# A gated state-space and feed-forward kernel on one core: the order of the feed-forward pieces inside the steps of the scan

## The reference

```python
# layer 1, for each sequence; z = layernorm(x)
u     = silu(conv(in_proj_w @ ctx) + conv_b)
dt_lo, Bm, Cm = x_proj_w @ u
delta = softplus(dt_proj_w @ dt_lo + dt_proj_b)
state = state * exp(delta_t * A) + (delta_t * u_t) * B_t      # over t, 256 channels x 16 states
y     = sum_n state * C_t;  y = (y + D * u) * silu(z)
x     = x + tanh(g_xattn) * y
# layer 2; act_quant: per token, scale = 128 / max|x|, rounded; weight_quant: ternary
h     = layernorm(x)
inter = silu(act_quant(h) @ wq_gate.T) * (act_quant(h) @ wq_up.T)
x     = x + tanh(g_ffn) * (act_quant(fwht(inter)) @ wq_down.T)   # fwht: Walsh-Hadamard over 1024
```

## Time and profile before

| | us |
|---|---|
| median of 3 runs (lowest, highest) | 287.43 (285.79, 288.03) |
| the profiled execution's own time | 287.4 |
| its span, first to last instruction | 285.6 |
| DVE busy (share of the span) | 211.9 (74%) |
| PE busy | 202.8 (71%) |
| ACT busy | 157.5 (55%) |
| POOL busy | 146.9 (51%) |
| mean granted clock of TensorE, as a share of full speed | 0.831 |

### The profile page before, as it was taken

One profiled execution on the slowest core, in us unless ns is written; L12 is line 12 of the kernel. 1 busy time (PEld: TensorE's weight loads), 2 busy tenths in 40 slices (PEclk: granted clock), 3 DMA queues, 4 the chain that ended last, 5 costly groups with the idle time before them and its releaser, 6 DMA issues. The chain is left out here.

```text
span 285.6 us, 3700 instructions
## 1 busy us (share of the span) xinstructions
PE 202.8 (71%) x1216; PEld 164.9 (58%) x1216; DVE 211.9 (74%) x340; ACT 157.5 (55%) x271; POOL 146.9 (51%) x213
## 2 busy tenths in 40 slices
PE   3779499936796976478595865695959646493856
PEld 2467389924684964367484743484848435372744
DVE  4399997839999984659696946497969355669872
ACT  1677979594045969732866579115773600651140
POOL 1101954999620685599795054999300098306600
PEclk9999755985797799989869599779886959979595
DMA  2990000000000000000000000000000000000001
GB/s 55 297 346 11 0 3 0 1 2 0 0 0 2 0 1 2 1 0 0 2 0 18 0 3 0 18 1 2 0 18 2 1 0 21 0 0 1 18 21 37
DMA packets 8149, 6.34 MB, mean 22 GB/s; under 512 B 2202, under 2 KB 7874, under 8 KB 8130
## 3 DMA queue, kind: packets, MB, share of 16 engines
q1 hardware_dynamic: 7154, 6.02, 6.5%
q10 hardware_dynamic: 976, 0.09, 0.2%
HBM read 5.05 MB, written 1.05 MB: 21 GB/s over the span
## 5 line engine op out<-in xcount | busy, mean ns | idle before, releaser
L1094 POOL TENSOR_SCALAR driveT<-duT,BT 128x256 f32<-128x256 f32 x120 | 61.1, 531 | 41.5 <-ACT duT L828 17.2
L811 ACT ACTIVATE decay<-delta,zero_c,aneg 128x255 f32<-128x255 f32 x128 | 65.4, 588 | 4.4 <-DVE state L1219 2.7
L458 PE MATMUL PY<-id,prod 128*128 128x128 f32 x256 | 44.3, 331 | 3.4 <-DVE prod L1261 1.9
L404 PE MATMUL BC<-id,driveT 128*128 128x128 f32 x120 | 23.4, 330 | 31.0 <-DVE state L1219 31.0
L458 PEld LDWEIGHTS PY<-id,prod 128*128 128x128 f32 x256 | 39.2, 175 | 5.4 <-issue 2.3
L1119 POOL TENSOR_TENSOR wnat<-wnat 128x512 f32<-128x512 f32 x18 | 22.8, 1267 | 36.8 <-DVE wnat L1341 36.0
L1219 DVE TENSOR_TENSOR_SCAN state<-decay,BC 128x512 f32<-128x512 f32 x30 | 36.4, 1212 | 3.5 <-issue 3.1
L1261 DVE TENSOR_TENSOR prod<-state,BC 128x1024 f32<-128x1024 f32 x32 | 38.2, 1195 | 0.0
L404 PEld LDWEIGHTS BC<-id,driveT 128*128 128x128 f32 x120 | 17.1, 174 | 34.1 <-issue 27.0
L1219 DVE TENSOR_TENSOR_SCAN state<-decay,UP 128x512 f32<-128x512 f32 x30 | 35.8, 1194 | 0.0
L1341 DVE SCALAR_TENSOR_TENSOR wnat<-GP,us,wq 128x1024 f32<-128x1024 f32 x7 | 9.0, 1283 | 30.0 <-issue 30.0
(11 more groups left out here) (205 smaller groups left out, 409.0 us busy)
## 6 DMA issues: line engine op xcount, KB each, us to landing
wnat<-in_L_ffn_w_gate_dram SPq DMA_DIRECT2D x1, 1024.0 KB, 9.6
xs<-in_x_dram SPq DMA_DIRECT2D x1, 1024.0 KB, 12.0
wnat<-in_L_ffn_w_up_dram SPq DMA_DIRECT2D x1, 1024.0 KB, 11.9
wnat<-in_L_ffn_w_down_dram SPq DMA_DIRECT2D x1, 1024.0 KB, 11.3
out_dram<-ot SPq DMA_DIRECT2D x8, 128.0 KB, 1.7
ctxs<-in_ctx_dram SPq DMA_DIRECT2D x1, 384.0 KB, 7.1
ctxs<-in_ctx_dram SPq DMA_DIRECT2D x1, 128.0 KB, 2.9
inw<-n_L_xattn_in_proj_w_dram SPq DMA_DIRECT2D x1, 128.0 KB, 2.7
```

Source lines behind the costliest of these rows:

```text
L404: last = nc.tensor.transpose(drive_bank(h)[:, L * n + P * c:L * n + P * (c + 1)], driveT[:, m % RING, c, n, P * h:P * (h + 1)], id32[:])
L458: last = nc.tensor.matmul(PY[:, E * c + P * h:E * c + P * (h + 1)], prod[:, g % RING, h, n, P * c:P * (c + 1)], id32[:], is_transpose=True ...
L811: last = nc.scalar.activation(decay[:, m % RING, h, n, 1:L], delta[:, b % 2, h, 1:L], ACT.Exp, bias=zero_c[:], scale=aneg[:, h, NB * j + n ...
L1094: last = nc.gpsimd.tensor_scalar(driveT[:, m % RING, c, n], duT[:, b % 2, c], BT[:, b % 2, c, NB * j + n:NB * j + n + 1], 1.0, ALU.mult, A ...
```

## The change

The order of pieces inside the steps changes on DVE, PE and ACT; POOL's and SP's programs stay, and so do the number and the shapes of all instructions. On DVE several pieces now stand between the scans and the product of a step instead of ahead of the scans or behind the product; the product comes later in these steps. On PE tokens_T moves ahead of `C_rows` of step 3, the gates go to step 3, up 0 to step 4, up 1 and down 1 to step 5, q2_T and down of half 0 one step later. On ACT rstd2 goes to step 1, the silus to step 3 behind its decays, tokens_out_early ahead of them, and q2_out_early 0 behind the decays of step 2. For f = 0 the transposed tokens go to bank6 instead of X, and four waits are changed to fit the new order.

```diff
--- before.py
+++ after.py
...
     return bank6 if k == 0 else X
+
+def tokens_bank(f):
+    return bank6 if f == 0 else X
...
             pe.wait_ge(act_BT, 2)
-        else:
-            pe.wait_ge(act_qT, n - 1)
+        elif n == 2:
+            pe.wait_ge(act_conv, 2)
+        else:
+            pe.wait_ge(act_qT, 2)
         for h in range(HALF):
...
         if f == 0:
-            pe.wait_ge(act_conv, 2)
-        if f + 1 < B:
+            pe.wait_ge(dve_wT, 6)
+        elif f + 1 < B:
             pe.wait_ge(act_szT, f + 2)
...
             for h in range(HALF):
-                last = nc.tensor.transpose(X.bitcast(BF16)[:, L * h + P * c:L * h + P * (c + 1)],
+                last = nc.tensor.transpose(tokens_bank(f).bitcast(BF16)[:, L * h + P * c:L * h + P * (c + 1)],
                                            q[:, c, P * h:P * (h + 1)], id16[:])
...
                 pe.wait_ge(dve_out, LC * f + t)
+            else:
+                pe.wait_ge(act_qT, 1)
         elif (f, t) == (B - 2, 0):
...
                 drive_rows(g + 2, 1)
+            if s == 3:
+                if new:
+                    tokens_T(f)
             if g + 1 < B * STEPS:
...
                     inter_T(p, 1)
+            if s == 2:
+                if old:
                     q2_T(p, 0)
-            if s == 2:
                 if front:
...
                     hadamard_mm(p, 1)
+            if s == 3:
+                if k == 0:
+                    du_T(1)
+                if old:
                     down(p, 0)
-            if s == 3:
+                if new:
+                    gate(f, 0)
                 if front:
                     in_proj(n, 1)
-                if k == 0:
-                    du_T(1)
-                if new:
-                    tokens_T(f)
+                if new:
+                    gate(f, 1)
             if s == 4:
...
                 if new:
-                    gate(f, 0)
-                    gate(f, 1)
+                    up(f, 0)
                 if old:
...
                 if new:
-                    up(f, 0)
+                    up(f, 1)
+                if old:
+                    down(p, 1)
             if s == 6:
...
                     weight_T(5)
-                if new:
-                    up(f, 1)
-                if old:
-                    down(p, 1)
                 if front:
...
         act.wait_ge(pe_qT, f + 1)
-        nc.scalar.copy(qT[:], X.bitcast(BF16)[:, 0:HALF * L].rearrange("p (h l) -> p h l", h=HALF)
+        nc.scalar.copy(qT[:], tokens_bank(f).bitcast(BF16)[:, 0:HALF * L].rearrange("p (h l) -> p h l", h=HALF)
                        ).then_inc(act_qT, 1)
...
             g = STEPS * k + s
-            if s == 0:
-                if new:
-                    rstd2(f)
             if s == 1:
...
                     gate_out(0)
+                if new:
+                    rstd2(f)
                 if old:
...
             if s == 2:
-                if old:
-                    q2_out_early(p, 0)
                 if new:
...
             if s == 3:
+                if new:
+                    tokens_out_early(f)
                 if old:
                     quant_down(p, 1)
+            if s == 4:
+                if k == 0:
+                    copy_duT(1)
             if s == 5:
...
                     q2_out_early(p, 1)
-            if s == 4:
-                if k == 0:
-                    copy_duT(1)
             if s == 7:
...
                     gate_out(k)
+            if s == 2:
+                if old:
+                    q2_out_early(p, 0)
             if s == 3:
+                if new or k + 1 < B:
+                    for_silu()
+                if new:
+                    silu_gate(f, 0)
                 if front:
                     conv_out(n)
-                if new:
-                    tokens_out_early(f)
+                    silu_u(n)
+                if k + 1 < B:
+                    silu_z(k + 1)
+                if new:
+                    silu_gate(f, 1)
+                for_exp()
             if s == 4:
...
                     copy_duT(k + 1)
-                if new or k + 1 < B:
-                    for_silu()
-                if new:
-                    silu_gate(f, 0)
-                if front:
-                    silu_u(n)
-                if k + 1 < B:
-                    silu_z(k + 1)
-                if new:
-                    silu_gate(f, 1)
-                for_exp()
             if s == 7:
...
             if s == 1:
-                if new:
-                    stats2(f, dve_ln_link.begin(dve, f))
                 if k == 0:
                     split(1)
-                if old:
-                    absmax2(p, 0)
+            if s == 2:
+                if old:
+                    round_down(p, 0)
             if s == 3:
-                if old:
-                    result(p, 0)
-                    absmax2(p, 1)
+                if new:
+                    round_tokens(f)
+            if s == 4:
+                if old:
+                    round_down(p, 1)
+            if s == 5:
+                if k == 0:
+                    weight_round(1)
             if s == 6:
-                if new:
-                    gate_times_up(f, 0)
-            if s == 7:
-                if new:
-                    gate_times_up(f, 1)
-                if old:
-                    result(p, 1)
+                if k == 0:
+                    weight_round(2)
             if g + 1 < B * STEPS:
...
                 scan(g + 1, 1)
+            if s == 1:
+                if old:
+                    absmax2(p, 0)
+                if new:
+                    second_rstd(f, dve_ln_link)
+            if s == 2:
+                if k == 0:
+                    weight_means()
+                if new:
+                    token_scale(f, dve_ln_link)
+            if s == 3:
+                if old:
+                    absmax2(p, 1)
+            if s == 4:
+                if k == 0:
+                    weight_round(0)
+                if old:
+                    result(p, 0)
+            if s == 5:
+                if k == 0:
+                    weight_out(0)
+                    weight_out(1)
+                if new:
+                    gate_times_up(f, 0)
+            if s == 6:
+                if k == 0:
+                    weight_out(2)
+                    weight_out(3)
+                if new:
+                    gate_times_up(f, 1)
+                if old:
+                    result(p, 1)
+            if s == 7:
+                if k == 0:
+                    weight_out(4)
+                    weight_out(5)
             times_C(g)
...
                     residual(f)
+                    stats2(f, dve_ln_link.begin(dve, f))
                 if 1 <= k < B - 1:
...
                     weight_abs(2)
-            if s == 1:
-                if new:
-                    second_rstd(f, dve_ln_link)
-                if old:
-                    round_down(p, 0)
-            if s == 2:
-                if k == 0:
-                    weight_means()
-                if new:
-                    token_scale(f, dve_ln_link)
-            if s == 3:
-                if new:
-                    round_tokens(f)
-                if old:
-                    round_down(p, 1)
-            if s == 4:
-                if k == 0:
-                    weight_round(0)
-                    weight_round(1)
-            if s == 5:
-                if k == 0:
-                    weight_out(0)
-                    weight_out(1)
-                    weight_round(2)
-            if s == 6:
-                if k == 0:
-                    weight_out(2)
-                    weight_out(3)
-            if s == 7:
-                if k == 0:
-                    weight_out(4)
-                    weight_out(5)
```

More of the change, by code:

```diff
@@ L1507, in _ @@
                             weight_out(5)
+                    times_C(g)
+                    if s == 0:
+                        if new:
+                            residual(f)
+                            stats2(f, dve_ln_link.begin(dve, f))
+                        if 1 <= k < B - 1:
+                            split(k + 1)
+                        if k == 0:
+                            weight_abs(2)
             p, f = B - 2, B - 1
```

12 lines of the change are left out of this document (3 added, 9 removed).

## The result

| | before | after |
|---|---|---|
| median of 4 runs, us | 287.41 | 267.12 |
| lowest to highest, us | 285.79 to 288.03 | 264.49 to 269.72 |
| ratio to before (95% interval) | | 0.922 (0.915 to 0.929) |
| forecast, range | | 266.2, 259 to 278 |

The same kernel was run again with the experiments: median 265.87 of 4 runs (263.69 to 266.87), ratio 0.923 (0.915 to 0.930), with a profile of 265.2 us (span 263.4).

The account below looks back on a forecast made before the run. DVE's in-order queue, standing still while a chain through PE and ACT catches up, was taken as the bound. Waits of 40.1 us less 12.9 new gave 27.2; less 5 (clock) and 1 (port), 21.2: from 287.4 to 266.2 us, range 259 to 278.

Parts of the forecast that it names:

- The bound and the waits that go: Blocks 1 to 3: DVE's in-order queue is the bound, and 40.1 us of its waits go.
- the walk: Piece-by-piece timing of each block through the queues: 40.1 us of waits go, 12.9 come, a gain of 27.2.
- the 2.6 ahead of second_rstd: Block 1 on DVE: new wait of 2.6 us, as second_rstd is reached at 91.2 and rstd2 ends at 93.8.
- The 3.4 ahead of the scan of step 5: Block 1 on DVE: new wait of 3.4 us, as the scan's drive rows stand behind gate 1 on PE.
- The lower level of the clock: PE pieces on the path running at 1.2 GHz: a deduction of 5 us, bounds 0 and 31.5.
- Rivals 1 and 4: 1: PE's queue takes half the gain back, 278 us, chance 0.14; 4: PE at 1.2 GHz wherever waited for, 293, 0.04.
- The 31.5 us: Upper bound of the clock deduction over three blocks: PE's path pieces at 1.2 GHz, some 10.5 us more a block.
- The port of DVE and POOL: round_down and round_tokens meet POOL more often: a deduction of 1 us, up to 1.04 each, bounds 0 and 7.
- the seven pieces that I had counted: DVE's round_down and round_tokens pieces, each of which could lose 1.04 us by meeting POOL.
- Rival 3: The wait only moves, to ahead of the scans of step 5 on DVE: 287 us, chance 0.05.
- rival 2: POOL's drives for steps 2 and 3 of the next block stand behind folds: 272 us, chance 0.08.
- a margin of 0.5 to 1: Slack in us the walk left for POOL's drives for steps 2 and 3 of the next block, queued behind folds.

Follow-up runs that it names:

- x2: Kernel before with only PE's and ACT's new orders, DVE's order kept except result of half 0 moved to step 4: 274.39 us, ratio 0.952.
- x1: Kernel before with only DVE's new order, gate_times_up and result of half 1 left at their old place: 287.20 us, ratio 0.989.
- x5: Changed kernel with gate 1 behind the drive rows of step 4 on PE: 266.99 us, ratio 0.929 to the kernel before.
- x7: Changed kernel with the edits of x4 and x6 together: 262.69 us, ratio 0.913 to the kernel before.
- x9: x7 with copy_duT moved ahead of the decays of step 4 on ACT: 259.57 us, ratio 0.899 to the kernel before.
- x6: Changed kernel with gate 0 right behind tokens_T on PE and the silus ahead of step 3's decays on ACT: 265.95 us, ratio 0.923.
- x4: Changed kernel with rstd2 ahead of softplus on ACT: 265.23 us, ratio 0.922 to the kernel before.
- x3: Changed kernel with gate_times_up and result of half 1 back ahead of the scans of steps 6 and 7: 264.70 us, ratio 0.919.

## Why the prediction was right, and where not

**The bound and the waits that go: right.** The 40.1 us of the earlier trace rows went almost whole from their places, and the larger new waits stand where the walk had put them. In the second profile, at a clock of 1.00 and 0.96 in blocks 2 and 3, the new waits add up to 6.8, 3.6 and 3.7 us against 6.6, 3.5 and 2.35 of the walk; in the first to 7.0, 6.1 and 5.2. Split behind stats2, the 2.6 ahead of second_rstd measured 2.65 and 2.97. The 3.4 ahead of the scan of step 5 measured 3.73 and 3.35.

**The lower level of the clock: of the right order.** I took 5 us for it. Over the walk's 12.45 the two profiles have 1.6 and 5.8 us more of waits. The difference of two executions of one kernel, 5.45 us in blocks 2 and 3, is the best measure here, and some of that is rounding time of DVE. Rivals 1 and 4, which let it eat the gain, did not come: the gates again ran mostly at the full level. The 31.5 us that I gave for PE at the lower level everywhere were therefore never put to the test.

**The port of DVE and POOL (the way into SBUF that the two share): mis-sized.** I took 1 us. The row of round_tokens at 101.37 took 1.78 (0.42 before), round_down at 186.32 took 1.71 (0.69), and the last piece of split at 133.47 took 1.09 (0.41 in block 1 of the same profile), each while POOL was at work. That is a loss per piece of up to 1.36, above the bound of 1.04 that I had set, and it fell on split too, which I had not counted.

DVE's busy time in the three cuts is 116.7 us against 113.0, 3.7 more. The rows of roundings and split account for 2.7 of it (2.3 for the seven pieces that I had counted, 0.45 for split). The other 1.0 is not in the length of any piece: consecutive rows overlap less than before, and why they do is open. In the first profile the rows account for 1.6 of 2.8.

So the terms were off one against the other, and it is partly luck that the total fits. In the second profile 39.6 of waits removed in the three blocks less 14.1 new, less 3.7, is 21.8; measured 21.3. In the first 39.6 less 18.3, less 2.8, is 18.5; measured 17.0, as waits too short for this list add up to more there.

POOL at work is not enough for a loss. Two roundings beside POOL's drives kept their time: round_down at 142.00 with 0.68 and round_tokens at 192.81 with 0.42; a third, in the first profile, did lose beside them (194.12, 1.30). With its usual duration taken off its end, the piece at 101.37 began in earnest at 102.73, the one at 133.47 at 134.15 and the one at 186.32 at 187.34 (estimates from the rows). Each time that is 0.1 us from the end of a POOL instruction with two inputs, at 102.85, 134.29 and 187.48.

The Trainium skill's rule (SBUF — State Buffer, "Who interferes with whom"), that a DVE instruction with two SBUF inputs contends with GpSimd's reads too, agrees with the row of split (both its inputs lie in SBUF): 1.09 beside POOL's fold, 0.41 alone. Scans and products kept their 1.2 us, as that rule has it for one input in PSUM.

**Block 1 gave less than the walk:** 1.9 us in one profile and 3.1 in the other, for a walk of 4.3. The 1.36 of round_tokens is over half of what is missing in the first case. As x2 shows, this block would be shorter with DVE's old order. Block 0 and the tail came as forecast: 0.4 us to the start of block 1 (1.2 in the first profile), and the tail at 43.9 and 44.4 against 44.4 before. PE's tail rows in the second profile:

```profile
224.72 1.09 PE L612 MATMUL GP<-id,wnat 128*128 128x128 f32 x8 [1.20 <-POOL wnat L1130]
228.17 0.40 PE L557 MATMUL X<-id,q 128*128 128x128 bf16 x4 [2.36 <-DVE q L1340]
```

inter_T of half 1 again stands behind POOL's last fold, 1.20 us now for 0.18, and tokens_T still comes 2.36 us after it is done: the cover was used but not used up.

**What I had not seen.** I gave the walk one sum and did not ask which half of the change earns it. Asked with x1, the same way of walking was 13 to 17 us wrong by the median (11 to 15 by the ratio): I let the gates and up 0 come too soon, and forgot that the accumulate ahead of each waits for a product in front of which the edit puts more of DVE's work. Rival 3, that the wait only moves, is what happens to DVE's half alone, and to x5. It is not what happens to the whole, since PE moves tokens_T and the gates ahead of that product at the same time.

**POOL's queue (rival 2)** costs the changed kernel little. PE waits for drives four times in the three blocks of the second profile, 5.4 us in all. Two of these waits, in blocks 2 and 3, are at the step where the walk left a margin of 0.5 to 1:

```profile
138.81 0.66 PE L407 MATMUL BC<-id,driveT 128*128 128x128 f32 x4 [1.06 <-POOL driveT L1104]
...
185.06 1.11 PE L407 MATMUL BC<-id,driveT 128*128 128x128 f32 x4 [2.89 <-POOL driveT L1104]
```

The scans that take these rows, at 142.60 and 187.95, do not wait. POOL's queue showed only when the silus were made quicker (x7, x9).

**What stays open:** why x6 by itself gained nothing while with x4 and the copy it is part of a gain of 6 us (x4 with the copy alone was not run); and what sets PE's clock level from one execution to the next, which is worth 4 to 5 us here and hides effects of that size in single profiles.

## What to carry to other kernels

Where engines run written-out queues against each other, walk the whole change through all queues: what an order is worth depends on the orders that feed it (DVE's gives 0.9 to 3.3 us alone and 8 to 9 on top of the others', and in block 1 it even costs time). A wait of a bottleneck engine names the place where the chain catches up with it, and moving the place (x3, x5) moves the wait; shortening the chain, and then looking at which queue has become late (x7, then x9), is what pays. The best order that the runs tell apart, x9, takes 259.6 us against 287.7 before in its session.

## What the runs showed of the hardware

One kernel, two executions: blocks 2 and 3 together took 94.8 us at granted clocks of 0.93 and 0.85, and 89.3 at 1.00 and 0.96. Adding matrix work, 0.87 us a step at 2.4 GHz and most of it where PE idled (x8), left the clock of these blocks at 0.93 and 0.96, within what the unaltered kernel shows; what sets its level is open.
